# Three moved settings in a three-layer graph attention kernel: when V of layer 1 is reduced, when a weight half is rounded, and at which layer tile the first shifts are turned

## The reference

```
x1   = relu(x @ W_ah + b_ah)
for l in 0..2:                       # every layer reads x1
    h    = (x1 @ W[l]) as (1250, 4, 192)
    e    = leaky_relu(sum(h * a_src[l])[src] + sum(h * a_dst[l])[dst], 0.2)
    p    = exp(e - max of e over the edges into dst)
    xs_l = relu(sum over edges of p / (sum of p) * h[src] + b[l])
out  = layernorm(x + relu(concat(xs_0, xs_1, xs_2) @ W_out + b_out))
```

## Time and profile before

| what | value |
|---|---|
| three timed runs | 936.89, 938.37, 938.94 us (median 938.37) |
| the profiled execution | 937.93 us |
| its span in the profile | 936.3 us |
| TensorE busy | 915.9 us, 98% of the span |
| VectorE busy | 748.4 us, 80% |
| ScalarE busy | 382.4 us, 41% |
| GpSimd busy | 45.8 us, 5% |

### The profile page before, as it was taken

One profiled execution on the slowest core, in us unless ns is written; L12 is line 12 of the kernel. 1 busy time (PEld: TensorE's weight loads), 2 busy tenths in 40 slices (PEclk: granted clock), 3 DMA queues, 4 the chain that ended last, 5 costly groups with the idle time before them and its releaser, 6 DMA issues.

```text
span 936.3 us, 14404 instructions
## 1 busy us (share of the span) xinstructions
PE 915.9 (98%) x5650; PEld 878.6 (94%) x5650; DVE 748.4 (80%) x1076; ACT 382.4 (41%) x586; POOL 45.8 (5%) x94
## 2 busy tenths in 40 slices
PE   6999999999999999999999999999999999999997
PEld 2678899999999999999999999999999999999996
DVE  6999957899899799999999999998877454343232
ACT  1578433222221435555555555555555631010000
POOL 4700000000000000010010010010010100000000
PEclk9999999999999999999999999999999999999999
DMA  5340626543542921352352351339541264233111
GB/s 176 50 133 38 190 74 212 184 159 87 163 160 79 261 96 42 96 147 60 96 122 57 98 136 43 96 84 333 164 124 42 77 155 164 83 113 122 47 34 33
DMA packets 57717, 108.31 MB, mean 116 GB/s; under 512 B 14020, under 2 KB 41257, under 8 KB 56502
## 3 DMA queue, kind: packets, MB, share of 16 engines
q1 hardware_dynamic: 39204, 66.24, 23.5%
q0 software_dynamic: 5360, 18.77, 7.8%
q10 hardware_dynamic: 13090, 22.44, 7.5%
HBM read 80.34 MB, written 27.10 MB: 115 GB/s over the span
## 4 chain that ended last, share of the span: by engine, by line
PE 57%; DVE 0%; ACT 0%; issue 0%; ACTq 0%
PE ps L1485 35%; PE ps L1568 18%; PE ps L1560 2%; PE ps L1520 2%; ACT R_XIN L832 0%; PE ps L1470 0%; DVE R_XIN L1264 0%; DVE stats L1254 0%; DVE R_EXP L1248 0%; DVE R_EXP L1250 0%; ACT rstd L892 0%; DVE mv L1259 0%; DVE rstd L1261 0%; ACTq L831 0%
## 5 line engine op out<-in xcount | busy, mean ns | idle before, releaser
L1485 PE MATMUL ps<-R_W 125*125 125x193 f32 x2400 | 396.0, 327 | 3.5 <-ACT R_XIN L821 2.2
L1485 PEld LDWEIGHTS ps<-R_W 125*125 125x125 f32 x2400 | 391.5, 188 | 4.7 <-ACT R_XIN L821 2.8
L806 ACT ACTIVATE R_W<-R_EXP,s 125x1250 f32<-125x1250 f32 x120 | 160.6, 1340 | 168.6 <-DVE R_EXP L1112 113.7
L1123 DVE SCALAR_TENSOR_TENSOR R_W<-R_W,R_CNT 125x1250 f32<-125x1250 f32 x120 | 174.5, 1455 | 3.0 <-DVE R_EXP L1112 2.0
L1153 DVE CUSTOM_DVE_ANT_0 R_ROWS<-R_MASK,R_ROWS 125x1250 bf16<-125x1250 bf16 x90 | 124.8, 1456 | 2.4 <-DMA R_ROWS<-as_dram 2.0
L1369 PE MATMUL ps<-Wl_hi,x_hi 128*125 128x392 f32 (+1 forms) x360 | 116.2, 341 | 0.0
L1369 PE MATMUL ps<-Wl_hi,x_lo 128*125 128x392 f32 (+1 forms) x360 | 115.6, 340 | 0.0
L1369 PE MATMUL ps<-Wl_lo,x_hi 128*125 128x392 f32 (+1 forms) x360 | 115.6, 339 | 0.0
L1568 PE MATMUL ps<-Wo_lo,xs_hi 128*125 128x384 f32 (+2 forms) x324 | 109.5, 338 | 0.0
L1568 PE MATMUL ps<-Wo_hi,xs_hi 128*125 128x384 f32 (+2 forms) x324 | 109.4, 338 | 0.0
L1568 PE MATMUL ps<-Wo_hi,xs_lo 128*125 128x384 f32 (+2 forms) x324 | 109.2, 337 | 0.0
(11 more groups left out here) (164 smaller groups left out, 894.1 us busy)
## 6 DMA issues: line engine op xcount, KB each, us to landing
xs_dram<-R_XIN POOLq DMA_DIRECT2D x18, 625.0 KB, 7.7
h_dram<-R_HOUT ACTq DMA_DIRECT2D x30, 336.0 KB
R_W<-h_dram SPq DMA_DIRECT2D x12, 840.0 KB
R_ROWS<-as_dram SPq DMA_DIRECT2D x12, 625.0 KB, 5.1
R_EXP<-u_dram SPq DMA_DIRECT2D x6, 1250.0 KB, 7.9
R_X<-u_dram SPq DMA_DIRECT2D x6, 1250.0 KB, 5.9
R_ROWS<-in_W_all SPq DMA_DIRECT2D x18, 384.0 KB, 4.1
Wo_sb<-in_W_out POOLq DMA_DIRECT2D x1, 6912.0 KB, 28.3
```

The costliest lines, as they stand in the source:

```text
L806: nc.scalar.activation(prob[r % PSLOTS], expo[:, r % XSLOTS], ACT.Exp, bias=s02[:, r % NT, ds(2 * p + r // NT, 1)]).then_inc(S["exp_done"], 1)
L1123: nc.vector.scalar_tensor_tensor(out=prob[r % PSLOTS], in0=prob[r % PSLOTS], scalar=HUGE, in1=cntT[:, r % NT, 0:N], op0=ALU.min, op1=ALU.m ...
L1485: ins = mm(ps[0:PT, o:o + HW], prob[(q * NT + j) % PSLOTS][:, t * PT:(t + 1) * PT], hB[:, q, j], start=(j == 0 and t % 2 == 0), stop=(j == ...
```

## The change

V of layer 1's third block is reduced before `more_counts` and not after it. ScalarE rounds the high part of the weights of part 1 after tile 4 of part 0, where it did after tile 5, and V of part 1 after tile 5, where it did after tile 8. TensorE turns the first shifts, and ScalarE copies them out, after tile 1 of part 5, where they did after tile 3. The edits of SyncE's ranges go with the new meaning of `V_TURN`; its order of loads is the same as before.

```diff
-V_TURN = 2
+V_TURN = 3
...
-V_NEXT_AT = (8, 3)
-ROUND_AT = 5
+V_NEXT_AT = (5, 3)
+ROUND_AT = (4,) + (5,) * 4
...
-U_AT = 3
+U_AT = 1
...
-            for k in range(VSLOTS - 1, V_TURN + 1):
+            for k in range(VSLOTS - 1, V_TURN):
                 load_v(1, k)
             sp.wait_ge(S["turn_ps"], x1_whole(2))
             sp.dma_start(w_raw[0], w_half(0)).then_inc(S["w_in_first"], 16)
-            for k in range(V_TURN + 1, V_TURN + VSLOTS):
+            for k in range(V_TURN, V_TURN + VSLOTS - 1):
                 load_v(1, k)
...
-            for k in range(V_TURN + VSLOTS, KT):
+            for k in range(V_TURN + VSLOTS - 1, KT):
                 load_v(1, k)
...
-                    if t == ROUND_AT and n < PARTS - 1:
+                    if n < PARTS - 1 and t == ROUND_AT[n]:
                         round_w(n + 1)
...
             for m in range(3, KT):
                 rest_wah(m)
-                if m - 3 < V_TURN:
+                if m < KT - 1:
                     reduce_v(1, m - 3)
             rest_v(0)
             rest_w(0)
+            reduce_v(1, V_TURN - 1)
             dve.wait_ge(S["turn_ps"], x1_whole(KT - 1))
             more_counts()
```

## The result

| kernel | median us | runs | ratio to the kernel before, 95% interval |
|---|---|---|---|
| before | 937.95 | 12 | |
| changed | 940.68 (940.16 to 941.59) | 12 | 1.0031 [1.0023, 1.0038] |

The change makes the kernel slower by 2.73 us (0.2 to 0.4%); 2.7 was forecast. The profiled execution took 941.59 us, 3.66 more than that of before, with a span of 940.0 us. So the profiled one lost 0.9 us more than the medians, and the reader should ask from the start where that lies. It is the slowest of the twelve.

A forecast was written before the change was run, and what follows sets the result against it. TensorE, busy 98% of the span, was taken as the bound. Waits of 0.4 us at `more_counts` and 2.3 at the transposes sum to 2.7 us, giving 940.6 or 941.1 by base; 940.9 was forecast, range 939.4 to 942.1.

The forecast's parts named there:

- Part 1: VectorE at `more_counts`: the moved V block delays the one-hots that TensorE awaits; cost 0.4 us, bounds 0 and 0.7.
- Part 2: VectorE from `more_counts` to the maxima: waits of 0.62 and 4.22 us go, maxima start 2.4 us sooner, at 169.0.
- Part 3: VectorE from maxima to `amax_done`: the 2.4 us lead is lost waiting for ScalarE at `rest_w(3)` and `rest_w(4)`; nothing left.
- Part 4: The transposes two tiles sooner: TensorE waits 2.3 us for `amax_done`, bounds 2.0 and 2.5; the attention stage gains 0.
- Gain 0: Start of the attention stage: `uB` arrives some 4 us sooner, but the first `exp` can't use it; three stalls stay.
- The first: Rival at the transposes: the maxima's lead survives, no wait, only 0.4 us lost, 938.8 us; chance 0.11.
- The one in which the attention stage profits: Rival: sooner shifts remove 2.8 us of TensorE's attention stalls while the transposes' wait stays, 938.3 us; chance 0.07.
- The clock rival: Rival behind the transposes' wait: the clock falls, one layer tile takes 3.17 us more, 944.1 us; chance 0.04.

The follow-up runs named there:

- experiment 1: The changed kernel with the transposes back after tile 3 of part 5 (`U_AT` 3): 937.87 us.
- experiment 2: The kernel before with only the transposes moved, to after tile 1 of part 5 (`U_AT` 1): 939.36 us.
- experiment 4: The changed kernel with eleven added matmuls, their result never read, ahead of TensorE's wait for `amax_done`: 940.64 us.
- experiment 5: The kernel before with only the third block of layer 1's V reduced ahead of `more_counts`: 937.82 us.
- experiment 9: The changed kernel with `round_w(3)` to `round_w(5)` one tile sooner, head 9's score row loaded before the shifts' store, head 1's second features and head 10's row after part 5: 937.83 us.
- experiment 3: The changed kernel with `round_w(3)` and `round_w(4)` one tile sooner on ScalarE: 941.43 us.
- experiment 6: The changed kernel with `round_w(3)`, `round_w(4)` and `round_w(5)` all one tile sooner on ScalarE: 940.50 us.
- experiment 7: The changed kernel with the loads of head 1's features and the source scores of heads 9 and 10 put off until part 5 is finished: 945.46 us.

## Why the prediction was right

**The time.** 2.7 us were forecast in sum and 2.73 measured. The larger part of the cause is right too: with the transposes put back the loss is gone (experiment 1), and they alone make most of it (experiment 2). But that the two numbers agree to a few hundredths is luck. Two terms were off in opposite directions, and a third was missing. The terms of the traces add up to more than the medians show: 0.6 + 2.07 + 1.5 = 4.2 us for the profiled execution, and 0.6 + 2.07 + 0.7 = 3.4 us for one like experiment 4, where the store's wait takes the place of the clock. In experiments 1, 2, 5 and 9 as well the medians show 0.2 to 0.5 us less than the traces do. Where this part goes is open; the runs of one kernel scatter by more.

**Part 1, the block.** Forecast 0.4, bounds 0 and 0.7; 0.6 in the traces (1.01 - 0.40), and only half of it for the reason given. The first instruction behind the reading of the counts started 1.68 us after the block's end, of the 2.0 us that the reading was put at: some 0.3 us of it lay beside the block. Measured from TensorE's first layer matmul (122.45 us before, 121.92 after), that instruction came 0.34 us later than before, which is the forecast's mechanism and near its size. The other 0.27 us arise behind it, between lines 960 and 961: they start 0.48 us apart, with 0.31 us of idle between them, where before it was 0.22:

```profile
124.87 0.18 DVE L961 TENSOR_SCALAR R_EXP<-R_EXP 128x16 f32<-128x16 f32 x1
```

All eight kernels with the block have this gap and none of the six without. The prediction has no term for it, and its cause is open. The Trainium skill's rule ("Perfetto Trace Analysis", "DVE / Act Engine Instruction"), that the sequencer hands an instruction on and is ready for the next, does not carry over to this wait with a reading behind it: by it the cost was 0, and the traces have 0.6 us in all eight kernels with the block.

**Part 2.** The waits of 0.62 and 4.22 us went, SyncE's second store left at 161.03 (forecast 161.0), the maxima started at 169.42 (169.0): 2.0 us sooner, not 2.4. V of layer 2 started at 152.60 where 151 was estimated, because the vectors took 6.8 us from their issue at 145.84 to arrive and not 5.

**Part 3.** As forecast: waits of 1.73 and 2.63 us at the two gates, the shifts' end moved by 0.07 us. The sentence that from 248.09 on VectorE works "without a gap that ScalarE could close" holds for this kernel alone, by a slack of 0.4 us (rounding done at 279.78, `rest_w(5)` at 280.20): experiment 3 ran into this third gate, `round_w(5)`.

**Part 4.** The wait was forecast at 2.3, bounds 2.0 and 2.5, and is 2.07: the hand-over to TensorE took 0.11 us after the shifts' end and not 0.34. "Gain 0" is right in what it denies: the first `exp` starts 0.13 us behind tile 7's stores as before, `uB`'s sooner arrival is used by nobody, and in experiment 9, with no wait at all, nothing is won. It is wrong as a bound from below. Sooner loads stand ahead of the stores of h, and the copy of tile 8 waited 1.61, 2.48, 2.55 and 4.54 us for them in experiments 2, 3, 4 and 6. That costs TensorE nothing in 2, 0.6 to 0.7 us in 3 and 4, and 2.6 us in 6.

**The rivals.** The first, no wait at the transposes and 938.8 us, was priced too low for that reason: experiment 6 is its mechanism (no wait at the transposes) and took 940.5. Its 938.8 needs the loads moved as well (937.8 in experiment 9). The one in which the attention stage profits is out. The clock rival, at 0.04, came true in the profiled execution, and by their times perhaps in up to half of the runs, so its chance was far too small; yet its price of 3.17 us was too high. The argument that a row must show it before it counts was the error there: TensorE's longest wait since the start-up was 1.1 us, so no row could tell. In size it was 1.5 us on the tiles and, against experiment 4, whose clock did not fall, 0.8, as the store's wait was paid there instead. The Trainium skill ("TensorE: Matmul & The Clock Gate", "What's actually happening") has the throttled state as the default, which activity releases. The traces agree that the clock can fall behind an idle stretch; it did not behind each one: 1.91 us twice with a fall, 1.92 and 1.75 without.

## What to carry to other kernels

Before a consumer is moved sooner, follow its producer through every gate on the way, also the one that shows no wait now, since it may have no slack; and follow the transfers that it sets off, since they will stand ahead of others that now pass first. A gap that is worth filling is found at the consumer: three instructions moved from the first tiles of attention into idle time gave 2.2 us, while three edits ahead of gates that other engines set gave nothing. The price of an idle TensorE isn't only its length: look at the clock in stretches of a microsecond behind it, because forty slices of a page will not show it.

## What the runs showed of the hardware

- The granted clock fell from 1.00 to 0.50 for some 3 us behind a wait of TensorE of 1.91 us, with full work ahead of it, in the traces of the changed kernel and of experiment 7, and behind waits of 3.41 us (experiment 6) and 3.52 us (experiment 7, in the attention stage); it did not behind 1.92 us in experiment 2 and 1.75 us in experiment 3. What decides between them is open.
- The store of two tiles of h (0.38 MB, two issues) was done 10 to 13 us after its issue (experiments 2, 3, 4 and 6) when SyncE's loads (1.25 MB for `uB`, 1.9 MB of h, 1.25 MB of score rows) had been issued within the 11 us ahead of it, with a DMA share of mostly 0.8 to 1.2. In the changed kernel, where the first of these loads stood 12 us ahead, it was done within 9.1 us; with the loads apart (experiment 9) within 3 us, since nothing moved from 312 to 315 us.
- The two issues of part 5's last store on ScalarE, 0.81 to 0.83 us in 13 traces, took 2.04 us in one (experiment 1) and delayed the `exp` behind them by as much, 1.2 us.
- A first instruction behind a loop's counts is followed 0.48 us later by the next in the eight kernels whose VectorE had a block of short instructions right ahead of the wait, and 0.22 us later in the six without. The cause is open.
